# A decoder layer on one core: maxima turned beside the value products, value products taken by four units, a fifth probability buffer

## The reference, cut to what matters

```python
x = x + attention(layernorm(x))        # 16 heads of 32 dims, causal over 512 tokens, then @ Wo
x = x + head_attention(layernorm(x), ctx, ctx)   # per token: 16 heads of 16 dims attend to 16 heads
x = x + ffn(layernorm(x))              # 4-bit quantised 256x256 weight, bias, low-rank term

scores = q @ k.T / sqrt(16)            # causal
probs  = softmax(scores)               # needs a maximum per query
out    = probs @ v
```

## Time and profile before

| | |
|---|---|
| time, median of 3 runs | 820.2 us (820.03 to 820.55) |
| span of the profiled execution | 819.2 us |
| PE busy | 769.2 us (94%) |
| DVE busy | 631.8 us (77%) |
| POOL busy | 472.8 us |
| ACT busy | 402.6 us |
| one batch in the steady part (420.70 to 506.92) | 86.2 us |

### The profile page before, as it was taken

One profiled execution on the slowest core, in us unless ns is written; L12 is line 12 of the kernel. 1 busy time (PEld: TensorE's weight loads), 2 busy tenths in 40 slices (PEclk: granted clock), 3 DMA queues, 4 the chain that ended last, 5 costly groups with the idle time before them and its releaser, 6 DMA issues.

```text
span 819.2 us, 16261 instructions
## 1 busy us (share of the span) xinstructions
PE 769.2 (94%) x5757; PEld 528.7 (65%) x5757; DVE 631.8 (77%) x1251; ACT 402.6 (49%) x760; POOL 472.8 (58%) x428
## 2 busy tenths in 40 slices
PE   8788999999999999999999999999999997998998
PEld 7555565765566566666666666665766674477996
DVE  3544555457769897899879997999788989699874
ACT  5123555555555466646746573646464556542111
POOL 5000000031966789677868686878876796976442
PEclk9997999999999999999999999999999999999999
DMA  5886666866685668566756675667567670100001
GB/s 186 111 104 89 94 78 84 136 84 85 86 136 78 91 85 135 71 91 105 92 100 89 103 92 100 88 103 95 85 86 110 85 110 8 60 14 7 33 14 39
DMA packets 47982, 70.56 MB, mean 86 GB/s; under 512 B 4898, under 2 KB 22579, under 8 KB 47923
## 3 DMA queue, kind: packets, MB, share of 16 engines
q1 hardware_dynamic: 46898, 69.52, 56.7%
q10 hardware_dynamic: 1024, 0.26, 0.2%
HBM read 14.98 MB, written 4.19 MB: 23 GB/s over the span
## 4 chain that ended last, share of the span: by engine, by line
PE 59%; DMA 18%; DVE 13%; issue 4%; ACT 3%; POOL 1%; SPq 1%; ACTq 0%; DVEq 0%; POOLq 0%
PE misc L524 21%; DMA stack_k<-k_lo 17%; PE exp_bank L524 15%; PE acc_bank L524 10%; PE max_bank L524 9%; PE sum_bank L524 3%; DVE neg_max L1225 2%; DVE score_rows L1237 2%; DVE seg_max L1225 1%; DVE ln_raw L1203 1%; SPq L455 1%; DVE head_out L1237 1%; ACT max_row L903 1%; PE misc L574 1%; DVE k_lo L1231 1%
## 5 line engine op out<-in xcount | busy, mean ns | idle before, releaser
L950 ACT ACTIVATE probs<-exp_bank 128x512 f32<-128x512 f32 x320 | 188.4, 592 | 199.6 <-PE exp_bank L524 196.8
L1225 DVE TENSOR_REDUCE neg_max<-max_bank 128x1 f32<-128x512 f32 (+1 forms) x192 | 130.2, 683 | 88.9 <-PE max_bank L524 88.0
L1600 POOL TENSOR_TENSOR prod<-head_probs,ctx_sb 128x256 f32<-128x256 f32 (+1 forms) x100 | 185.0, 1883 | 2.2 <-POOL head_probs L1595 0.5
L524 PE MATMUL max_bank<-stack_k,stack_q 96*128 96x384 f32 (+3 forms) x512 | 155.2, 364 | 16.7 <-DMA stack_k<-k_lo 9.4
L524 PE MATMUL acc_bank<-probs,values 128*32 128x512 f32 (+3 forms) x1024 | 158.5, 447 | 4.1 <-ACT log_sum L961 2.1
L314 POOL TENSOR_TENSOR prod<-x1n,ctx_sb 128x256 f32<-128x256 f32 (+1 forms) x104 | 158.8, 1558 | 4.3 <-ACT x1n L910 4.3
L524 PE MATMUL sum_bank<-probs,ones 128*32 128x512 f32 (+3 forms) x1024 | 157.8, 444 | 0.0
L524 PE MATMUL exp_bank<-stack_q,stack_k 97*128 97x384 f32 (+3 forms) x512 | 149.3, 354 | 2.0 <-DVE wf_lo L1195 1.3
L524 PEld LDWEIGHTS exp_bank<-stack_q,stack_k 97*128 97x128 f32 x512 | 83.9, 194 | 56.4 <-issue 27.4
L1540 POOL TENSOR_TENSOR ln_var<-ln_mv,eps 128x4 f32<-128x4 f32 x21 | 4.4, 212 | 196.1 <-DVE ln_mv L1211 196.1
L1225 DVE TENSOR_REDUCE seg_max<-max_bank 128x4 f32<-128x512 f32 x128 | 86.8, 683 | 29.6 <-PE max_bank L524 27.8
(11 more groups left out here) (185 smaller groups left out, 1413.4 us busy)
## 6 DMA issues: line engine op xcount, KB each, us to landing
stack_q<-q_hi SPq DMA_DIRECT2D x64, 256.0 KB, 5.1
stack_k<-k_hi SPq DMA_DIRECT2D x64, 256.0 KB, 9.5
stack_q<-q_lo SPq DMA_DIRECT2D x32, 256.0 KB, 7.0
stack_k<-k_lo SPq DMA_DIRECT2D x32, 256.0 KB, 10.8
x_in<-in_x SPq DMA_DIRECT2D x9, 512.0 KB, 5.5
ctx_sb<-in_ctx SPq DMA_DIRECT2D x32, 128.0 KB, 3.1
x<-in_x SPq DMA_DIRECT2D x7, 512.0 KB, 10.1
out<-y_sb SPq DMA_DIRECT2D x5, 512.0 KB, 3.3
```

What stands on the lines that cost most here:

```text
L524: return nc.tensor.matmul(*args, **kw)
L950: nc.scalar.activation(probs[:, (UNITS * g + n) % PTR, :], exp_bank[n % 2][:, :], ACT.Exp, scale=SCALE).then_inc(exp_done, 1)
L1225: vec.tensor_reduce(o, v, axis=AX_X, op=ALU.max, negate=True).then_inc(max_taken, 1)
L1600: last = gp.tensor_tensor(pv_prod[:, COFF[j]:COFF[j + 1]].rearrange("p (q d k) -> p q d k", q=4, k=keys), head_probs[:, 4 * j:4 * j + 4, N ...
```

## The change

`turn_maxima` moves from unit 1 to unit TURN = 5, in front of the value products there, for all passes with i >= 0; ACT's side, `send_maxima`, goes to the end of its unit 4. The value products are called with units 0 to 3 at n = 5 and units 4 to 7 at n = 9; units 8 and 9 stay at n = 1. `probs` gets a fifth buffer, and the exponential of unit n waits for the value products of unit n - 5. The waits for `v_ready` and `acc_saved` move with the first value products from n = 3 to n = 5.

```diff
-    PTR = 4
+    PTR = 5
+    TURN = 5
@@ PE
+            def turn_maxima_of(st):
+                if st["M"]:
+                    turn_maxima(st["M"][1])
...
                         if stack_early(i, g) and n == 1 and (i, g) != FIRST_PASS:
-                            if i >= 0:
-                                turn_maxima(st["M"][1])
                             for which in (0, 1):
                                 project_qk(st["A"][1], which)
...
                         if st["C"]:
-                            if n == 3:
+                            if n == TURN:
+                                turn_maxima_of(st)
                                 if g % 2 == 0:
                                     pe.wait_ge(v_ready, n_v.up(2))
                                 wait(pe, acc_saved, n_acc.up() - 1)
-                            if n in (3, 5, 7, 9):
-                                attend((n - 3, n - 2), st["C"][1], first_tile)
+                            if n in (5, 9):
+                                attend(range(n - 5, n - 1), st["C"][1], first_tile)
...
-                        if st["M"] and n == 1 and i >= 0 and not stack_early(i, g):
-                            turn_maxima(st["M"][1])
@@ ACT
+            def send_maxima(m_slot):
+                act.wait_ge(max_psum, n_row.up())
+                wait(act, max_stacked, n_row_free.up(16) - 32)
+                copy(max_row[:, m_slot % 2, :], misc[0][0:G * NT, 0:P]).then_inc(max_row_ready, 1)
+                wait_apart(act, const_ready, (max_row_ready, n_row.now()))
+                nc.scalar.dma_start(stack_q[STACK:STACK + 1, m_slot, :, :].bitcast(F32),
+                                    max_row[:, m_slot % 2, :].bitcast(F32)).then_inc(max_stacked, 16)
...
-                        if st["M"] and n == 1:
-                            m_slot = st["M"][1]
...
+                        if st["M"] and i < 0 and n == 1:
+                            send_maxima(st["M"][1])
...
+                        if st["M"] and i >= 0 and n == TURN - 1:
+                            send_maxima(st["M"][1])
```

## The result

The changed kernel takes 863.13 us (median; 862.14 to 865.79), the kernel before 820.12 beside it: ratio 1.0518 (1.0497 to 1.054). It is 5.2% slower where 1.7% faster was forecast, and 43 us above the upper end of the range. The profiled execution spans 863.9 us against 819.2.

What follows compares the result with a forecast made beforehand. PE was taken to set the pace, stack DMAs second. Batches 0 to 2 -8, batches 3 to 6 -5, batch 7 -1: together -14, span 805, 806 us with 1.0 around it, 1.7% faster; range 789 to 820.

Steps and rivals of the forecast that it cites:

- the third rival: Row of maxima, issued amid the stacks, lands late: at 10.9 us 31 passes lose over 4 us each, above 920; chance 0.01.
- 18.3 us as the shortest pass: Stack transfers, 14.35 us, plus 3.96 us to the next first issue without the turn: no pass can be shorter.
- The steady batch without the row's wait: Batches 3 to 6: turn saves 2.9 us, other terms add 1.65, net -1.25 of 86.2 us each.
- The turn: Transpose leaving unit 1 lets the projection start 0.72 us earlier: 21.6 us over 30 waits, 3 us back at its new place.
- The ways of the value products: Products by four save two ways in and out of the 32-column shape per pass, 0.25 us each: 16 us.
- The late exponentials: Fifth buffer one too few: exponentials 5 to 7 up to 1.3 us late in 13 passes; g = 3 +0.25, g = 1 +0.1.
- `project_v` behind the turn in g = 0: From batch 3 on, the value projection waits for ACT's copy of the maxima in `misc[0]`, 1.1 us late.
- The logarithm's 2.1 us: PE's two waits for ACT's logarithm, 2.1 us, fall away with two units more of slack.
- Batches 0 to 2: No second layernorm, less DVE work, paced by the stacks: together 8 us saved.
- The tail: Batch 7, no projections after its first pass: nothing for the turn, +1.4 - 0.7 in g = 0, -1.5 in g = 2: -1 us.
- stack waits stay or grow: Sign in PE's waits: those for `stack_k<-k_lo`, among 9.4 us in 13 stack waits, stay or grow.
- it is wrong if the odd passes keep their length: Sign against the forecast: passes g = 3, 19.03 us before, should measure 18.3 to 18.7 us.

Runs made afterwards that it cites:

- e7: Changed kernel with value products by pairs, four buffers, and the three k stack copies issued after the row of maxima: 818.07 us, ratio 0.9949 to the kernel before.
- e8: Changed kernel with value products by pairs and four buffers, stack copies from batch 1 on cut to a sixteenth of their bytes: 824.14 us, ratio 1.0004.
- e3: Changed kernel with each stack copy from batch 1 on cut to a sixteenth of its bytes, same number of transfers: 825.6 us, ratio 1.0065.
- e6: Changed kernel with the three k stack copies of a pass issued only after ACT's copy of the row of maxima: 821.93 us, ratio 0.998.
- e10: Changed kernel with value products by pairs, five buffers, k stack copies behind the row except in g = 0, turn at unit 6 there: 811.36 us, ratio 0.988.
- e2: Kernel before with only the value products by four units and the fifth buffer, the turn left at unit 1: 830.11 us, ratio 1.0132.
- e9: As e10, but value products by four units in passes g = 1 and 2: 809.19 us, ratio 0.9847 to the kernel before.
- e5: Changed kernel with only the last stack copy of a pass (`k_lo`) issued after ACT's copy of the row of maxima: 840.34 us, ratio 1.0267.

## Why the prediction was wrong

**The step that failed** is the third rival, the row that lands late, and its 0.01. The mechanism was named, and its number was read wrongly from the earlier trace rows. There the row had 4.2 us of landing and the stack copy 10.9, and I took 4.2 as the time a row needs among stack traffic. But they had been issued apart, as SP's and ACT's timelines of the kernel before have it:

```profile
50.76 0.56 SPq L455 DMA_DIRECT2D stack_k<-k_lo  x1
```
```profile
57.66 0.51 ACTq L968 DMA_DIRECT2D stack_q<-max_row  x1
```

57.66 + 4.2 = 61.86 and 50.76 + 10.9 = 61.66. The row landed with the last stack copy already then, and 4.2 was merely what was left of the copy's way. The rule to be read from that pair was "it lands when what is ahead of it has landed", not "4.2 us". With it the outcome could be seen: the landing is then needed at unit 0 of the next pass and no longer at unit 1, which makes a pass g = 3 20.9 us where it was 18.8 to 19.0. The rule of the Trainium skill on which I leaned ("DMA: Bandwidth & Descriptors", Queues, rings and completion order: an engine goes round its queues packet by packet) would let a small transfer on another queue pass; the packets of the row, of which none moved before SP's packets issued ahead were all but through (first one 7.1 us after the issue with six copies ahead, 4.9 with five), don't show that, and the measurement decides. In the kernel before all but a few rows went out ahead of the stacks (median 1.8 us), so the trace held next to nothing about the row's new place; a chance of 0.01 could not rest on one pair of rows.

**Its price** was wrong the other way. "Above 920" supposed a landing of 10.9 us, 6.3 of it covered, so that each of 31 passes loses over 4 us. The median landing was 9.0, and in the pass shown PE had work until 553.39, 7.1 us after the issue: it waited 1.7. Besides, the landing of the last stack copy had held up the passes' unit 1 before too, so only the difference between the two places counts: 1.3 us a pass on average.

**Where the floor lay.** 18.3 us as the shortest pass is borne out where the stacks set the pace and the row is not late: the pass g = 2 of batch 1 takes 18.2 us in e7, with a wait for `stack_k`, and 17.4 in e8, with the small stacks. In the steady passes g = 3 the 18.3 us that e7 shows are no proof of it: e8 takes 18.3 there too, so something else sets them. For the changed kernel the chain was the same, but it ends at unit 0 and makes 20.9.

**The steady batch without the row's wait** was forecast at 84.95 us, and e3 measures 85.0. e6, whose transfers are whole, takes 85.1 in batch 3 but 86.6 and 86.2 in batches 4 and 5, so its mean of 86.0 is hardly below the 86.2 before. That e3 hits it is partly luck, as the terms show:

- The turn, 0.72 us a pass: e10 shows 1.5 us a batch, 0.4 a pass. Of PE's waits 2.2 us went and 1.0 came, as shown above. The rest of the 0.72, some 0.28 a pass or 1.1 a batch between the turn and its follower, hardly went: PE's busy time fell from 82.82 to 82.66. That the transpose costs it at its new place too would fit, but no run took the transpose away.
- The ways of the value products, 0.5 us a pass. This term was too large. A steady batch of e2 has the kernel before with two ways fewer in each of four passes, and PE's busy time (the third number; before, then e2) falls by 1.07 us, 0.27 a pass:

```profile
397.02:483.24 86.22, 82.89 (x638) 55.18 (x637) 76.47 (x148) 48.65 (x94) 65.72 (x54) 1.00 0.67 98
```
```profile
397.85:484.07 86.22, 81.82 (x638) 55.70 (x637) 73.59 (x148) 48.61 (x94) 65.67 (x54) 1.00 0.67 98
```

  e9 against e10 gives 0.3 a pass in the same way, and its 0.6 of length is half idle time. Four units take 546.69 - 544.84 = 1.85 us where 2.05 was forecast. The estimate by the Trainium skill's drain, 0.2 us a pass, was nearer than the 0.5 that I took. In e2 even the 1.07 us did not shorten the batch: new waits ate them (14.7 us for exponentials).
- The late exponentials: forecast up to 1.3 us in 13 passes. The wait is there, 13.0 us in 25, at most 0.8. From turn to turn e6's pass g = 3 takes 19.45 us and e7's 18.33: fours lose 1.1 us there, forecast 0.25. In g = 1 they win 1.0 (18.69 against 19.69), forecast -0.1. By passes the forecast was wrong, in the sum right, in the batches of e6 that nothing else disturbs.
- `project_v` behind the turn in g = 0: forecast 1.1 us late, measured 5.6 us in 6 waits, at most 1.1 (one of them ahead of the first batch). Right.
- The logarithm's 2.1 us: no wait for it stands among those of the changed kernel. Right.

**Batches 0 to 2** were to win 8 us; e6 wins 9.3 (239.0 against 248.3 us), so this was right too, once the row is out of the way.

**The tail** was to win 1 us and loses 7.0; in e6, where the row doesn't matter, 7.5, and batch 6 another 5.8. This is the second error, and it explains why e6 is at 822 and not at 806: -9.3 -0.6 +5.8 +7.5 = +3.4 against the forecast of -14. (The profiled execution of e6 is the slowest of its ten, 2.6 us above the median, so these two losses are rather large in it.) In those passes PE idles for ACT and DVE and then gets a lower clock, as e2's rows show (0.93, 0.78). The tail before and in e6:

```profile
654.53:819.20 164.67, 150.99 (x1098) 118.67 (x1097) 132.72 (x289) 59.44 (x113) 106.93 (x112) 0.99 0.16 35
```
```profile
650.49:822.70 172.21, 156.01 (x1099) 121.85 (x1098) 132.31 (x289) 59.49 (x114) 104.71 (x110) 0.96 0.15 34
```

PE's busy time is 5.0 of the 7.5 us, at a clock of 0.96 instead of 0.99, and idle time 2.5. The forecast had a price for waiting, none for the clock that follows it.

**Of the other signs named beforehand**, "stack waits stay or grow" was wrong (9.4 to 5.3 us, since the row's wait stands ahead of them), and "it is wrong if the odd passes keep their length" was met: 20.9 us where 18.3 to 19 was expected.

**What stays open**: why the row waits for bytes of another queue. The runs show that it is bytes (e3) and that the row's packets move once those issued before it on the other queue are all but through (the changed kernel, e5), not whether the row is held in the DMA engines or ahead of them. And which waits lower the clock in e9's tail (168.0 against 165.7) was not taken apart.

## What to carry to other kernels

A small transfer that someone waits for should be issued ahead of the large ones; issued behind them, on another queue too, it cost here what was left of them. When a step with a DMA moves within a loop, compare landing instants (issue plus duration), not durations: two transfers that end together may mean that one waits for the other, and the instants of their packets settle it. And price a moved wait by the difference between the old and new first waiter, plus the clock that PE may lose when it idles again in every pass, as it did in batch 1 here.

## What the runs showed that I had not expected

- An 8 KB transfer on ACT's queue took 9.0 us (median) behind 1.5 MB of SP's, 7.4 with one 256 KB transfer fewer ahead, 3.4 with three fewer, 1.8 where the transfers were a sixteenth in size. Its packets began to move only as those of the copies issued before it ran out.
- The granted clock fell where PE idled only a little more: 0.92 in three passes in a row, the first with 3.5 of 22.65 us idle, 1.00 in those with 1.0 of 18.78, and 1.00 in a single one with 3.1 of 20.90. In the tail 2.7 us of idle time in 12 us went with 0.78 in the 6 us behind.
- Cutting nearly all bytes of the stack copies in the kernel before gave 0.65%, although PE's waits for them were 9.4 us and DMA had 18% of the chain.
